# The last four routing tiles of a two-layer cross-attention kernel taken step by step together

## The chip, the cores and the metric

One Trainium2 chip, one of its cores. The metric is device time in microseconds (us) of one execution of the whole kernel. The kernel before was timed three times.

## The reference

x has 2048 rows of 256 numbers, the context 1601 rows of 192. Layer 0 routes the context into x and passes the result through a gate; layer 1 is a block of self-attention, cross-attention and MLP. All of it is f32. The part that the change touches is layer 0 and the start of layer 1:

```python
tok = context @ W_proj + b_proj
attn = softmax(x @ tok.T / 16)
routed = attn @ tok
ps_n, in_n = ln(x), ln(routed)
u = sigmoid([ps_n, in_n] @ W_u + b_u)
r = sigmoid([ps_n, in_n] @ W_r + b_r)
cand = tanh([r * ps_n, in_n] @ W_n + b_n)
x1 = ln((1 - u) * x + u * cand)
h = ln(x1)                      # layer 1
q, k, v = h @ wq.T, h @ wk.T, h @ wv.T
...
```

Then come 16 heads of width 16 over 2048 keys, a cross-attention over the 1601 context rows, and an MLP of width 1024.

## The kernel before

The order of every engine's work is written out by hand, and engines wait for one another with counting semaphores. The 2048 rows are 16 **tiles** of 128 rows in 4 **chunks** of 512. Layer 0 runs as a pipeline of **slots**, one per tile. In the slots 0 to 15 TensorE makes scores and weighted context sums of a chunk (`l0_scores`, `l0_pv`), and among them, four slots behind, the steps of a tile:

- `route` (L1094, L1095): two accumulating matmuls give the routed row sums in PSUM bank 6.
- `norms` on VectorE (L1701 to L1714): reciprocal of the row sum, scaling of the routed rows (L1702), their statistics, an inverse root (`rsqrt`, L1496 to L1503: 3 small instructions and 3 times 3 more, each waiting for the one before, for up to three columns at once: the routed tile, the new state of an earlier one, the finished x1 of a third), then the normalised routed row (L1709) and the normalised x1 of a third tile (`XH1`, L1714).
- `hats` (L1103): four transposes into bank 3; `concat` on ScalarE (L792) puts them into `CF`.
- `gates` (L1113, L1116): 16 and 8 matmul records into bank 7; `reset` (L771) and `update` (L777) are their tanh on ScalarE, the vector `gates` (L1723, L1725) lie between.
- `candidate` (L1125) in bank 7 again, its bias on VectorE (L1746, `CZ`), its tanh on ScalarE (L799, `CD`), then the new state `E2` (L1750 to L1752) and its statistics (L1512, L1514).
- `finish` (L1734, L1736): x1 from the new state, and its statistics. `h_transposed` (L1024, bank 2) and `h_taken` (L736) turn the normalised x1 into `hF`, from which layer 1 projects.

The buffers `TR`, `RPS`, `UZ`, `TU`, `CZ`, `CD`, `E2` exist once, `CF` and `XHS` twice. Slots 16 to 22 have no more scores: there the last tiles run one after the other, slot by slot.

The projections of layer 1 (`qkv`) are ten entries for each chunk, numbered 10n to 10n+9: two k units, two v units, a q unit, the norm of k, the second q unit, two v units, the norm of q. A k or q unit (L1042) is one eighth of a key or query projection, 128 features of 512 rows; a v unit (L1039) one tile. `split` on ScalarE evicts a k or q unit in three passes (L674, L675, L676: value, rounded value, square) and VectorE makes the lower part (`lower_parts`, L1536), after which GpSimd stores both. The squares buffer `SQ` has two halves, one for each unit of a pair. So a split first waits until the norm (L926) of the pair before has read them:

```python
wait(act, S["norms"], u // 2)
```

VectorE takes the norm of k (L1542, `k_norm`) and that of q (L1672, L1673). After the last norm of k it makes the row of shifts for the first queries (`self_shift(0)`, L1656 to L1519). Chunk 0 is projected behind slot 10, chunk 3 behind slot 22 (`DENSE`), chunks 1 and 2 in parts within the slots 16 to 21 (`EARLY`, `LATE`). Units 10 and up rotate over the PSUM banks 0, 1, 4, 5.

Behind all that `decide` computes a flag (L1834 to L1839, with L1228 on TensorE). TensorE loads it as a number and branches (`general`), and then starts the scores of the self-attention (L1308). GpSimd stores the parts of all chunks first and then the four rows of shifts; SyncE loads the keys and the first queries as those arrive.

Of the kernel before, what the change touches and what calls it, by code (L numbers as in the profile page):

```python
# [14 lines left out]
P = 128  # L15
# [116 lines left out]
def build(nc, ctx, d, out):  # L132
# [87 lines left out]
    TU = m.put("TU", [P, D], F32, oWOP + 3 * D * 4)  # L220
    PS = ctx.enter_context(nc.psum_tensor("PS", [P, 8, CHUNK], F32))
# [21 lines left out]
    AGX, NYX, MXP, NMX = 192, 224, 256, 272  # L243

    def sm(o, n=1, p=P):
# [10 lines left out]
        l0_scores l0_exp l0_lo l0_pv l0_oc l0_routed l0_hat l0_hatT l0_concat  # L256
# [44 lines left out]
    for n in range(CHUNKS):  # L301
        vs = [("v", kt, 0, 0) for kt in range(n * TPC, (n + 1) * TPC)]
        ks, qs = ([(kind, n * CHUNK, CHUNK, mm) for mm in range(2)] for kind in "kq")
        norms = [("norm", CHUNKS + 2 * n + i, CHUNK, 0) for i in range(2)]
        stage3.append([(10 * n + i,) + e for i, e in
                       enumerate(ks + vs[:2] + qs[:1] + norms[:1] + qs[1:] + vs[2:] + norms[1:])])
# [6 lines left out]
    DENSE = {10: 0, 22: 3}  # L313
    FIRST, SECOND = stage3[1], stage3[2]
    EARLY = {16: FIRST[0:4], 17: FIRST[8:10], 21: SECOND[8:10]}
    LATE = {16: FIRST[4:8], 19: SECOND[0:4], 20: SECOND[4:8]}
    SLOTS = TILES + TPC + 3
# [293 lines left out]
    def _(gp):  # L611
# [30 lines left out]
        for i in range(CHUNKS):  # L642
# [6 lines left out]
        for i in range(CHUNKS):  # L649
            store_shift(i, 0, i * CHUNK)  # L650
# [15 lines left out]
    def _(act):  # L666
# [99 lines left out]
        def reset(i):  # L766

            act.wait_ge(S["l0_gates"], i + 1)
            wait(act, S["l0_rps"], i)
            for c in range(2):  # L770
                ins = act.activation(TR[:, c, :], PS[:, 7, c * P:(c + 1) * P], ACT.Tanh, bias=sm(BRH + c), scale=0.5)  # L771
            ins.then_inc(S["l0_rtanh"], 1)

        def update(i):

            act.wait_ge(S["l0_ubiased"], i + 1)
            act.activation(TU[:], UZ[:], ACT.Tanh, scale=0.5)  # L777

        def state_hat(i):
# [5 lines left out]
            act.activation(XHS[:, i % 2, 0, :], X[:, i, :], ACT.Identity, scale=sm(NYX + i), bias=sm(NMX + i))  # L785

        def concat(i):

            act.wait_ge(S["l0_hatT"], i + 1)
            for k, (g_, b_) in enumerate(2 * [("L0_xattn_g_state", "L0_xattn_beta_state")]  # L790
                                         + 2 * [("L0_xattn_g_input", "L0_xattn_beta_input")]):
                ins = act.activation(CF[:, i % 2, k, :], PS[:, 3, k * P:(k + 1) * P], ACT.Identity,  # L792
# [3 lines left out]
        def candidate(i):  # L796

            act.wait_ge(S["l0_candz"], i + 1)
            act.activation(CD[:], CZ[:], ACT.Tanh).then_inc(S["l0_cand"], 1)  # L799

        def slot(k):
# [4 lines left out]
            if b >= CHUNKS:  # L806
                if k == TILES:
                    routed_out(b - 1)
                if g is not None:
                    reset(g)  # L810
                qkv(EARLY.get(k, ()))
                if g is not None:
                    update(g)
                state_hat(tile_at(k, 3))
                if r is not None:
                    concat(r)
                if g is not None:
                    candidate(g)
                qkv(LATE.get(k, ()))
                if h is not None:  # L820
                    h_taken(h)
                return
# [26 lines left out]
            else:  # L849
                if j == TPC - 1 and b + 1 < CHUNKS:  # L850
                    shift_row(b + 1)
                state_hat(tile_at(k, 3))
# [7 lines left out]
        for k in range(SLOTS):  # L860
            slot(k)
            if k in DENSE:
                qkv(stage3[DENSE[k]])

# [56 lines left out]
    def _(pe):  # L921
# [164 lines left out]
        def route(i):  # L1086
# [6 lines left out]
            wait(pe, S["l0_hat"], i)  # L1093
            pe.matmul(PS[:, 6, 0:D + 1], OC[:, 0, tt * P:(tt + 1) * P], WN[:, 0, :], start=True, stop=False)  # L1094
            pe.matmul(PS[:, 6, 0:D + 1], OC[0:SUM + 1, 1, tt * P:(tt + 1) * P], WN[0:SUM + 1, 1, :],  # L1095
                      start=False, stop=True).then_inc(S["l0_routed"], 1)

        def hats(i):
# [3 lines left out]
            for k in range(4):  # L1102
                ins = pe.transpose(PS[:, 3, k * P:(k + 1) * P], XHS[:, i % 2, k // 2, (k % 2) * P:(k % 2 + 1) * P],  # L1103
                                   ident[:])
            ins.then_inc(S["l0_hatT"], 1)

        def gates(i):

            pe.wait_ge(S["l0_concat"], i + 1)
            wait(pe, S["l0_candz"], i)  # L1110
            for mm in range(2):
                for c in range(4):
                    pe.matmul(PS[:, 7, mm * P:(mm + 1) * P], W0[:, 1, c, mm * P:(mm + 1) * P], CF[:, i % 2, c, :],  # L1113
                              start=(c == 0), stop=(c == 3))
            for c in range(4):
                ins = pe.matmul(PS[:, 7, D:2 * D], CF[:, i % 2, c, :], W0[:, 0, c, :], start=(c == 0), stop=(c == 3))  # L1116
            ins.then_inc(S["l0_gates"], 1)

        def candidate(i):
# [3 lines left out]
            pe.wait_ge(S["l0_rps"], i + 1)  # L1123
            for c in range(4):
                ins = pe.matmul(PS[:, 7, 0:D], RPS[:, c, :] if c < 2 else CF[:, i % 2, c, :], W0[:, 2, c, :],  # L1125
                                start=(c == 0), stop=(c == 3))
            ins.then_inc(S["l0_candps"], 1)

        def slot(k):
# [4 lines left out]
            if b >= CHUNKS:  # L1134
                if k == TILES:
                    for i in range(LAG):
                        l0_pv(n - LAG + i)
                    route(r)
                if g is not None:
                    gates(g)  # L1140
                qkv(EARLY.get(k, ()))
                if r is not None:
                    hats(r)
                if g is not None:
                    candidate(g)
                if tile_at(k, 3) is not None:
                    route(r + 1)
                qkv(LATE.get(k, ()))
                if h is not None:
                    h_transposed(h)  # L1150
                return
# [57 lines left out]
        for k in range(SLOTS):  # L1209
            slot(k)  # L1210
            if k in DENSE:
                if DENSE[k] == 0:
                    pe.wait_ge(S["saw_loaded"], 64)
                qkv(stage3[DENSE[k]])
# [878 lines left out]
```

## Time and profile before

| | us |
|---|---|
| three runs | 1514.67, 1515.40, 1518.74 |
| median | 1515.40 |
| the profiled execution | 1512.68 |
| its span, first to last instruction | 1511.0 |
| TensorE busy | 1409.6 (93%) |
| VectorE busy | 567.5 (38%) |
| ScalarE busy | 1094.8 (72%) |
| last layer 0 sum ends, by the span's clock | 322.8 |
| first self-attention score starts | 435.2 |
| mean granted clock of TensorE | 0.968 |

The span is the time between the first and the last recorded instruction; 1.7 us of the execution lie outside it. The granted clock is a share of full speed. Rows of a timeline give the start (us from the span's start), the busy time (us), the engine, the line, the operation, what it writes and reads, its size and count, and in square brackets the idle time of the engine before it with what ended that.

### The profile page before, as it was taken

What the parts mean: (1) busy time and instruction counts of PE and PEld (TensorE: products, weight loads), DVE (VectorE), ACT (ScalarE), POOL (GpSimd) and SP (SyncE); (2) the same over time, 40 slices, a digit from 0 to 9 for tenths busy, and PEclk for the clock granted to TensorE, in tenths of its full rate; (3) what the DMA queues carried; (4) which work ended last, traced back from release to release, by engine and by line L of the source; (5) the groups of instructions that cost most, each with busy time, mean ns of one, the idle gap of its engine ahead of it and who ended that gap; (6) DMA issues with size and microseconds to landing.
All of it is one profiled execution on the core that took longest, in us unless ns stands there. A gap on an engine that the chain in (4) does not pass through costs nothing.

```text
span 1511.0 us, 20524 instructions
## 1 busy us (share of the span) xinstructions
PE 1409.6 (93%) x7934; PEld 623.1 (41%) x7934; DVE 567.5 (38%) x1343; ACT 1094.8 (72%) x1346; POOL 48.7 (3%) x63
## 2 busy tenths in 40 slices
PE   7989899996679999999999998998999999999988
PEld 5668676775422223223222322322323432432347
DVE  5557575777540113303322231440431233143132
ACT  2543444453359999998999998888877787788842
POOL 2000000010010000000000000000000000000000
PEclk9999999998789999999999999999899999999998
DMA  9410001001269000100100353501000000000000
GB/s 298 164 37 1 1 1 56 1 29 51 88 125 148 22 13 12 39 14 15 34 28 12 44 119 48 122 29 47 12 12 15 22 12 12 22 15 1 4 11 14
DMA packets 35048, 66.05 MB, mean 44 GB/s; under 512 B 6203, under 2 KB 20093, under 8 KB 34205
## 3 DMA queue, kind: packets, MB, share of 16 engines
q1 hardware_dynamic: 29580, 43.24, 13.3%
q0 software_dynamic: 5360, 21.37, 3.9%
q8 instruction: 69, 1.13, 0.3%
q14 instruction: 39, 0.31, 0.1%
HBM read 42.70 MB, written 22.02 MB: 43 GB/s over the span
## 4 chain that ended last, share of the span: by engine, by line
PE 67%; ACT 21%; DVE 6%; issue 3%; DMA 2%; SPq 0%; DVEq 0%; POOL 0%; ACTq 0%; POOLq 0%
PE PS L1325 20%; ACT PX L886 19%; PE PS L1308 14%; PE PS L1376 4%; PE PS L1386 3%; PE PS L1361 2%; PE PS L1113 2%; PE PS L1125 2%; PE PS L1116 2%; PE PS L1042 2%; PE PS L1081 1%; PE PS L1082 1%; PE PS L1083 1%; PE PS L1344 1%; PE PS L1459 1%
## 5 line engine op out<-in xcount | busy, mean ns | idle before, releaser
L886 ACT ACTIVATE PX<-PS 128x1024 f32<-128x1024 f32 (+1 forms) x928 | 882.6, 1039 | 136.0 <-PE PS L1308 87.9
L1325 PE MATMUL PS<-PX,V 128*32 128x512 f32 (+1 forms) x3712 | 500.7, 612 | 5.0 <-ACT PX L886 3.0
L1308 PE MATMUL PS<-QST,stack 50*128 50x512 f32 (+1 forms) x1856 | 386.0, 474 | 19.6 <-issue 13.7
L1308 PEld LDWEIGHTS PS<-QST,stack 50*128 50x128 f32 (+1 forms) x1856 | 157.0, 185 | 417.5 <-ACT PX L886 335.5
L1882 DVE COPY OT<-PS 128x512 f32<-128x512 f32 x32 | 22.1, 691 | 310.5 <-PE PS L1325 309.3
L1325 PEld LDWEIGHTS PS<-PX,V 128*32 128x32 f32 (+1 forms) x3712 | 73.9, 108 | 151.3 <-issue 129.3
L755 ACT ACTIVATE PH<-PS 128x512 fp32r<-128x512 f32 (+1 forms) x52 | 31.2, 600 | 79.4 <-PE PS L1062 69.3
L1386 PE MATMUL PS<-W,HIDT 128*128 128x256 f32 x192 | 51.5, 414 | 9.8 <-ACT HIDT L872 9.8
L1376 PE MATMUL PS<-HC,W 128*128 128x512 f32 x96 | 53.2, 641 | 0.0
L1909 DVE RECIPROCAL REC<-REC 128x256 f32<-128x256 f32 x30 | 52.6, 1753 | 1.0
L771 ACT ACTIVATE TR<-PS,small 128x128 f32<-128x128 f32 x32 | 10.0, 363 | 56.7 <-PE PS L1116 56.7
L1386 PEld LDWEIGHTS PS<-W,HIDT 128*128 128x128 f32 x192 | 36.5, 200 | 34.5 <-issue 30.0
L1954 DVE TENSOR_SCALAR HIDT<-PS,cols 128x512 f32<-128x512 f32 x24 | 18.0, 751 | 79.9 <-PE PS L1376 79.8
L1694 DVE TENSOR_TENSOR PL<-PEXP,PH 128x512 fp32r<-128x512 f32 (+1 forms) x52 | 35.8, 689 | 27.2 <-ACT PEXP L756 26.1
L1081 PE MATMUL PS<-PH,CN 128*128 128x512 f32 (+1 forms) x104 | 43.2, 416 | 0.9 <-DVE PL L1694 0.9
L1932 DVE TENSOR_TENSOR XH<-PS,rows 128x256 f32<-128x256 f32 x28 | 11.9, 425 | 81.2 <-PE PS L1361 81.2
L1082 PE MATMUL PS<-PH,CN 128*128 128x512 f32 (+1 forms) x104 | 41.5, 399 | 0.0
L1083 PE MATMUL PS<-PL,CN 128*128 128x512 f32 (+1 forms) x104 | 41.4, 398 | 0.0
L1587 DVE TENSOR_REDUCE small<-PS 128x1 f32<-128x512 f32 x64 | 35.1, 570 | 8.2 <-PE PS L963 7.4
L1959 DVE TENSOR_TENSOR XH<-PS,rows 128x256 f32<-128x256 f32 x12 | 5.1, 425 | 78.2 <-PE PS L1386 78.2
L1042 PE MATMUL PS<-hF,SAW 128*128 128x512 f32 x64 | 31.5, 627 | 2.0 <-ACT hF L736 2.0
L792 ACT ACTIVATE CF<-PS,cols 128x128 f32<-128x128 f32 x64 | 24.0, 456 | 10.6 <-PE PS L1103 10.6
(194 smaller groups left out, 1461.6 us busy)
## 6 DMA issues: line engine op xcount, KB each, us to landing
QST<-q_parts SPq DMA_DIRECT2D x192, 64.0 KB
q_parts<-PARTS POOLq DMA_DIRECT2D x16, 512.0 KB, 3.6
stack<-k_parts SPq DMA_DIRECT2D x24, 200.1 KB, 6.7
stack<-k_parts SPq DMA_DIRECT2D x18, 256.0 KB
k_parts<-KPARTS POOLq DMA_DIRECT2D x8, 512.0 KB, 3.2
v_cross<-V POOLq DMA_DIRECT2D x1, 3328.0 KB, 12.3
V<-v_cross SPq DMA_DIRECT2D x2, 1664.0 KB, 13.7
k_parts<-PARTS POOLq DMA_DIRECT2D x6, 512.0 KB, 3.4
```

Source lines behind the costliest of these rows:

```text
L886: act.activation(PX[0:kr, (2 * t + half) % 4, :, :], PS[0:kr, slot:slot + 2, :], ACT.Exp, scale=SCALE).then_inc(at["exp"], 1)
L1042: ins = pe.matmul(PS[:, bank, :], SAW[:, "qk".index(kind), c, mm * P:(mm + 1) * P], hF[:, c, at:at + w], start=(c == 0), stop=(c == 1))
L1081: pe.matmul(PS[0:w, bank, :], c_hi, hi, start=first, stop=False)
L1082: pe.matmul(PS[0:w, bank, :], c_lo, hi, start=False, stop=False)
L1083: ins = pe.matmul(PS[0:w, bank, :], c_hi, lo, start=False, stop=last)
L1308: ins = pe.matmul(PS[0:kr, 2 * (n % LOOK) + jj, :], KST[a][lo:lo + NROW, pair, kt * P:kt * P + kr].bitcast(F32R), QST[lo:lo + NROW, pair, ...
L1325: ins = pe.matmul(PS[32 * j:32 * j + 32, 6, :], V[0:kr, kt, 2 * (g // 2 * GH + j) + g % 2, :], PX[0:kr, (2 * t + j // 2) % 4, j % 2, :], s ...
L1376: ins = pe.matmul(PS[:, 7, :], (CAWQ if kind == "u" else W1)[:, c, i * P:(i + 1) * P], HC[:, c, :], start=(c == 0), stop=(c == 1))
L1386: ins = pe.matmul(PS[:, 7, 0:D], HIDT[:, k, i * P:(i + 1) * P], W2[:, k, :], start=(k == 0), stop=(k == HID // P - 1))
L1587: ve.tensor_reduce(sm(MXP + tt * len(pcs) + p), PS[:, max_bank(m), 0:pcs[p][1]], AX, ALU.max) \
L1694: ve.tensor_tensor(PL[0:kr, n % RING, :].bitcast(F32R), PEXP[0:kr, n % RING, :], PH[0:kr, n % RING, :], ALU.subtract).then_inc(S["l0_lo"], 1)
L1909: ch(ve.reciprocal(part, part))
```

## The change

Slots 16 to 22 are replaced on every engine by a function `last_tiles` in which the tiles 12 to 15 go through each step together or close together. Their buffers (`CF4`, `XHS4`, `TR4`, `RPS4`, `TU4`, `CD4`, `E4`) exist four times, in the place of the context. Tile j of the four has a PSUM bank of its own for `route`, `gates` and `candidate` (6, 4, 5, 7). The statistics of the routed rows are made straight from PSUM, one inverse-root chain serves six columns, and ScalarE writes the normalised routed rows from PSUM. The new states of all four have one chain, and so have the four x1.

The projections of the chunks 1 and 2 have only the banks 0 and 1. The norm of k of chunk 1 stands behind `gates` of the last tile. In chunk 3 the values stand last, the norm of k comes forward by two units, and GpSimd stores the first row of shifts ahead of the last queries.

```diff
+        entries = ks + vs[:2] + qs[:1] + norms[:1] + qs[1:] + vs[2:] + norms[1:]
+        if n == CHUNKS - 1:
+            entries = ks + qs[:1] + norms[:1] + qs[1:] + vs[:2] + norms[1:] + vs[2:]
-    DENSE = {10: 0, 22: 3}
-    FIRST, SECOND = stage3[1], stage3[2]
+    DENSE = {10: 0}
+    FIRST, SECOND, THIRD = stage3[1:]
-        return (0, 1, 2, 3)[u % 4] if u < 10 else (0, 1, 4, 5)[u % 4]
+        return (0, 1, 2, 3)[u % 4] if u < 10 else u % 2 if u < 30 else (0, 1, 4, 5)[u % 4]
...
+                if half and i == CHUNKS - 1:
+                    store_shift(0, 0, 0)
```

ScalarE's new order:

```diff
+            a, b, c, e = LASTS
+            routed_out(CHUNKS - 1)
+            reset(a - 1)
+            update(a - 1)
+            for i in LASTS:
+                state_hat(i)
+            candidate(a - 1)
+            qkv(FIRST[0:1])
+            h_taken(a - 3)
+            qkv(FIRST[1:4])
+            for i in LASTS:
+                routed_hat(i)
+            concat(a)
+            concat(b)
+            reset(a)
+            update(a)
+            concat(c)
+            h_taken(a - 2)
+            reset(b)
+            update(b)
+            h_taken(a - 1)
+            candidate(a)
+            concat(e)
+            qkv(FIRST[4:5])
+            reset(c)
+            update(c)
+            candidate(b)
+            reset(e)
+            update(e)
+            qkv(FIRST[5:])
+            candidate(c)
+            candidate(e)
+            qkv(SECOND[0:6])
+            for i in LASTS:
+                h_taken(i)
+            qkv(SECOND[6:])
+            qkv(THIRD)
```

TensorE's:

```diff
+            for i in range(LAG):
+                l0_pv(STEPS - LAG + i)
+            gates(a - 1)
+            for i in (a, b, c):
+                route(i)
+            candidate(a - 1)
+            qkv(FIRST[0:1])
+            route(e)
+            h_transposed(a - 3)
+            qkv(FIRST[1:4])
+            hats(a)
+            hats(b)
+            gates(a)
+            hats(c)
+            h_transposed(a - 2)
+            gates(b)
+            h_transposed(a - 1)
+            candidate(a)
+            hats(e)
+            qkv(FIRST[4:5])
+            gates(c)
+            candidate(b)
+            gates(e)
+            qkv(FIRST[5:])
+            candidate(c)
+            candidate(e)
+            qkv(SECOND[0:6])
+            for i in LASTS:
+                h_transposed(i)
+            qkv(SECOND[6:])
+            qkv(THIRD)
```

VectorE's, with the two new helpers:

```diff
+        def routed_stats(i):
+            j = i - FIRST_LAST
+            ve.wait_ge(S["l0_routed"], i + 1)
+            ch(ve.reciprocal(sm(RS4 + j), PS[:, route_bank(i), D:D + 1]))
+            stats(PS[:, route_bank(i), 0:D], j, ch, STAT4, AG4)
...
+            for _ in range(2):
+                ch(ve.tensor_tensor(var, var, sm(RS4, TPC), ALU.mult))
+            rsqrt4(TPC + 2)
+            ch(ve.tensor_tensor(sm(SC4, TPC), sm(NY4, TPC), sm(RS4, TPC), ALU.mult))
+            ve.scalar_tensor_tensor(out=sm(SB4, TPC), in0=mean, scalar=-1.0, in1=sm(SC4, TPC), op0=ALU.mult,
+                                    op1=ALU.mult).then_inc(S["l0_scaled"], 1)
...
+            four = [(j, STAT4, AG4) for j in range(7)]
+            norms(None, a - 2, a - 3)
+            finish(a - 2, into=four[5])
+            gates(a - 1)
+            routed_stats(a)
+            routed_stats(b)
+            candidate_sum(a - 1)
+            routed_stats(c)
+            new_state(a - 1, four[4])
+            qkv(FIRST[0:1])
+            routed_stats(e)
+            routed_scales()
+            next_hat(a - 2, AG4 + 10, NY4 + 5)
+            finish(a - 1, AG4 + 8, NY4 + 4, four[6])
+            qkv(FIRST[1:4])
+            rsqrt4(1, 6)
+            next_hat(a - 1, AG4 + 12, NY4 + 6)
+            gates(a)
+            gates(b)
+            candidate_sum(a)
+            qkv(FIRST[4:5])
+            new_state(a, four[0])
+            gates(c)
+            candidate_sum(b)
+            new_state(b, four[1])
+            gates(e)
+            qkv(FIRST[5:])
+            candidate_sum(c)
+            new_state(c, four[2])
+            candidate_sum(e)
+            new_state(e, four[3])
+            rsqrt4(TPC)
+            qkv(SECOND[0:2])
+            for j, i in enumerate(LASTS):
+                finish(i, AG4 + 2 * j, NY4 + j, four[j])
+                qkv(SECOND[2 + j:3 + j])
+            rsqrt4(TPC)
+            for j, i in enumerate(LASTS):
+                next_hat(i, AG4 + 2 * j, NY4 + j)
+            qkv(SECOND[6:])
+            qkv(THIRD)
```

(a, b, c, e are the tiles 12, 13, 14, 15; `gates` and `candidate` on TensorE, and `reset`, `update`, `concat` on ScalarE, are as before but for buffers and banks.)

## Rows read from the trace of the kernel before

**Rows 1.** The page's first line.
```profile
span 1511.0 us, 20524 instructions
```

**Rows 2.** Windows: stretch, PE, PEld, DVE, ACT, POOL busy us (count), clock, DMA share, GB/s.
```profile
397.40:411.50 14.10, 3.19 (x12) 1.46 (x10) 10.77 (x39) 3.88 (x9) 1.45 (x2) 0.62 0.56 174
...
322.80:435.20 112.40, 76.09 (x316) 52.79 (x316) 73.50 (x225) 42.14 (x91) 13.24 (x15) 0.86 0.23 77
```

**Rows 3.** Timeline of slot 17 and the start of slot 18, VectorE and ScalarE.
```profile
354.50 0.42 DVE L1746 TENSOR_TENSOR CZ<-PS,rows 128x256 f32<-128x256 f32 x1 [1.27 <-PE PS L1125]
...
355.48 0.42 DVE L1750 TENSOR_TENSOR E<-CD,X 128x256 f32<-128x256 f32 x1 [0.55 <-ACT CD L799]
...
357.75 0.17 DVE L1701 RECIPROCAL small<-PS 128x1 f32<-128x1 f32 x1
357.95 0.48 DVE L1702 TENSOR_SCALAR E<-PS,small 128x256 f32<-128x256 f32 x1
358.58 0.43 DVE L1512 BATCH_NORM_STATS2 small<-E 128x6 f32<-128x256 f32 x1
...
359.38 0.17 DVE L1496 TENSOR_SCALAR small<-small 128x3 f32<-128x3 f32 x1
...
361.77 0.41 DVE L1709 TENSOR_SCALAR XHS<-E,small 128x256 f32<-128x256 f32 x1
...
363.59 0.48 DVE L1734 SCALAR_TENSOR_TENSOR E<-E,small,rows 128x256 f32<-128x256 f32 x1
...
363.94 1.48 ACT L792 ACTIVATE CF<-PS,cols 128x128 f32<-128x128 f32 x4
...
365.31 0.18 DVE L1514 BATCH_NORM_AGGREGATE small<-small 128x2 f32<-128x6 f32 x1
```

**Rows 4.** Timeline: ScalarE's split of the first query unit of chunk 1.
```profile
339.06 0.69 ACT L674 ACTIVATE PARTS<-PS,cols 128x512 f32<-128x512 f32 x1 [2.26 <-PE PS L926]
...
340.22 0.69 ACT L676 ACTIVATE SQ<-PS,cols 128x512 fp32r<-128x512 f32 x1
```

**Rows 5.** The chain that ended last: start, us, what, records merged.
```profile
334.16 1.73 PE PS L1125 x8
...
336.76 1.72 PE PS L1042 x4
...
341.75 1.79 PE PS L1113 x16
343.53 1.74 PE PS L1116 x8
```

**Rows 6.** Windows of 2 us around an idle TensorE (columns as in rows 2).
```profile
360.00:362.00 2.00, 0.00 (x0) 0.00 (x0) 1.69 (x10) 0.00 (x0) 0.00 (x0) 1.00 0.00 0
...
364.00:366.00 2.00, 2.00 (x6) 1.55 (x6) 1.17 (x4) 1.43 (x5) 0.00 (x0) 0.50 0.00 0
```

**Rows 7.** Timeline: the turn of tile 15 at low clock, and chunk 3.
```profile
409.83 0.69 PE L1024 MATMUL PS<-ident,XH 128*128 128x128 f32 x2 [4.24 <-DVE XH L1714]
...
411.57 5.08 PE L1042 MATMUL PS<-hF,SAW 128*128 128x512 f32 x8 [1.05 <-ACT hF L736]
```

**Rows 8.** Timeline: norm of k, shifts, values, the flag, the first score.
```profile
423.28 0.68 DVE L1542 TENSOR_REDUCE small<-PS 16x1 f32<-16x512 f32 x1
...
426.50 0.69 DVE L1536 TENSOR_TENSOR PARTS<-PARTS 128x512 fp32r<-128x512 f32 x1
427.23 0.76 DVE L1683 TENSOR_TENSOR V<-PS,rows 128x256 f32<-128x256 f32 x2
...
430.43 0.14 DVE L1839 TENSOR_SCALAR flag<-small 1x1 int32<-1x1 f32 x1
...
435.20 0.96 PEld L1308 LDWEIGHTS PS<-QST,stack 50*128 50x128 f32 x6 [5.13 <-issue]
```

**Rows 9.** The same turn into the cross-attention: flag, first score.
```profile
938.30 0.14 DVE L1839 TENSOR_SCALAR flag<-small 1x1 int32<-1x1 f32 x1
...
943.10 0.96 PEld L1308 LDWEIGHTS PS<-QST,stack 50*128 50x128 f32 x6 [5.15 <-issue]
```

More of the change, by code:

```diff
@@ L220, in build, with state_of, work_of, route_bank @@
     TU = m.put("TU", [P, D], F32, oWOP + 3 * D * 4)
+    FIRST_LAST = TILES - TPC
+    s = Map(nc, oKST + 2 * T * 4, oV)
+    CF4 = s.new("CF4", [P, TPC, 4, P], F32)
+    XHS4 = s.new("XHS4", [P, TPC, 2, D], F32)
+    TR4 = s.new("TR4", [P, TPC, 2, P], F32)
+    RPS4 = s.new("RPS4", [P, TPC, 2, P], F32)
+    TU4 = s.new("TU4", [P, TPC, D], F32)
+    CD4 = s.new("CD4", [P, TPC, D], F32)
+    E4 = s.new("E4", [P, TPC, D], F32)
+    assert s.at <= oKST + 2 * T * 4 + 2 * 4 * 2 * LPAD + 4 * LT * 2 * CW
+    def state_of(i):
+        if i < FIRST_LAST:
+            return CF[:, i % 2], XHS[:, i % 2]
+        return CF4[:, i - FIRST_LAST], XHS4[:, i - FIRST_LAST]
+    def work_of(i):
+        if i < FIRST_LAST:
+            return tuple(x[:] for x in (TR, RPS, UZ, TU, CZ, CD, E2))
+        j = i - FIRST_LAST
+        return TR4[:, j], RPS4[:, j], TU4[:, j], TU4[:, j], CD4[:, j], CD4[:, j], E4[:, j]
+    def route_bank(i):
+        return 6 if i < FIRST_LAST else (6, 4, 5, 7)[i - FIRST_LAST]
+    def gate_bank(i):
+        return 7 if i < FIRST_LAST else route_bank(i)
     PS = ctx.enter_context(nc.psum_tensor("PS", [P, 8, CHUNK], F32))
@@ L776, in update @@
             act.wait_ge(S["l0_ubiased"], i + 1)
[L777 removed]
+            _, _, uz, tu, _, _, _ = work_of(i)
+            act.activation(tu, uz, ACT.Tanh, scale=0.5)
         def state_hat(i):
@@ L805, in slot @@
             n = LT * b + (3 * j + 1 if j else 0)
[L806 to L822, printed above, removed]
             def piece(n):
@@ L858, in slot @@
                 h_taken(h)
-        for k in range(SLOTS):
+        for k in range(TILES):
             slot(k)
@@ L1133, in slot @@
             n = LT * b + (3 * j + 1 if j else 0)
[L1134 to L1151, printed above, removed]
             if j == 0:
@@ L1207, in slot @@
             maxima(5)
-        for k in range(SLOTS):
+        for k in range(TILES):
             slot(k)
@@ L1753, in candidate, with rsqrt4, routed_scales @@
-            stats(E2[:], 0, ch)
+            candidate_sum(g)
+            new_state(g)
+        def routed_stats(i):
+            j = i - FIRST_LAST
+            ve.wait_ge(S["l0_routed"], i + 1)
+            ch(ve.reciprocal(sm(RS4 + j), PS[:, route_bank(i), D:D + 1]))
+            stats(PS[:, route_bank(i), 0:D], j, ch, STAT4, AG4)
+        def rsqrt4(n, first=0):
+            rsqrt(n, ch, ag=AG4 + 2 * first, y=sm(NY4 + first, n), tmp=TMP4)
+        def routed_scales():
+            pairs = sm(AG4, 2 * TPC).rearrange("p (n two) -> p n two", two=2)
+            mean, var = (pairs[:, :, i:i + 1].rearrange("p n o -> p (n o)") for i in range(2))
+            for _ in range(2):
[4 more added lines that the diff above has]
+                                    op1=ALU.mult).then_inc(S["l0_scaled"], 1)
+            ve.wait_ge(S["l0_scaled"], 1)
@@ L1759, in slot @@
             n = LT * b + (3 * j + 1 if j else 0)
-            if b >= CHUNKS:
-                norms(r, f, h)
-                gates(g)
-                finish(f)
-                qkv(LATE.get(k - 1, ()))
-                qkv(EARLY.get(k, ()))
-                candidate(g)
-                return
             if j == 0:
@@ L1818, in slot @@
                 x_stats((None, range(6, 12), range(12, 16))[k])
-        for k in range(SLOTS):
+        for k in range(TILES):
             slot(k)
```

123 lines of the change are left out of this document (79 added, 44 removed).

## The prediction

> **What bounds the kernel now.** I read the page for the size of the stage, then windows, the timeline and the chain that ended last. The span is 1511.0 us [rows 1]; 1.7 us of the 1512.7 us execution lie outside it. The change touches 322.8 to 435.2, between the last sum of layer 0 and the first score of self-attention: 112.4 us in which TensorE is busy 76.1, VectorE 73.5 and ScalarE 42.1 [rows 2]. No engine is full. Work passes between them, and in 397.4 to 411.5 VectorE works 10.8 of 14.1 us while TensorE has 3.2. What follows 435.2 keeps its code, so I compute only when the first score starts. A change of 0.3% (4.5 us) is about what a measurement can tell from none.
>
> **Prices.** On VectorE, from start to start: an elementwise step 0.46 (0.42 busy and the gap behind it); CZ starts at 354.50 and the step behind its tanh at 355.48, so sum, tanh and waits are 0.98; a new state with statistics 357.75 - 355.48 = 2.27; reciprocal 0.20, scaling 0.63, statistics 0.80, so 1.63 up to 359.38; a root chain 361.77 - 359.38 = 2.39, or 0.20 for each of its 12 instructions; a finish with its statistics 363.59 to 365.5 = 1.9; a normalisation 0.45; `concat` 1.5 [rows 3]. A split takes 340.91 - 339.06 = 1.85, its pitch is 1.72, a 128x512 pass in it 0.58 [rows 4]. TensorE at full clock: candidate 1.73, a k or q unit 1.72, gates 1.79 + 1.74 = 3.53 [rows 5]; I take 0.86 for a v unit (half), 0.44 for four turned blocks, 0.22 for two, and 0.47 for a norm, scaled from these by columns.
>
> **What goes.** Seven root chains (slots 16 to 22) become five: 4.8 us less on VectorE. Four scalings of 0.63 go and four normalisations of 0.45 move to ScalarE: 4.3 less. Six small scale instructions come, 1.0 more with the later start. So VectorE loses some 8 us of work. On TensorE nothing goes. Whether this shows depends on the new order, which I walk.
>
> **Step A, 322.8 to 339.4.** TensorE starts gates of tile 11 at once, which hides the copy of the sums (a gain of 1.2). VectorE is the bound: from 323.0 chain 2.4, normalisation 0.45, finish 1.9, two gate steps 0.92, two routed statistics 2.0, CZ 0.46, a third 1.0, new state 2.27, a lower part 0.73, the fourth 1.0, joint chain and scales 3.2; sum 16.3. A statistic read from PSUM has no row; 0.43 as from SBUF, bounds 0.3 and 0.7 (the 512-wide reduction from PSUM is 0.68 [rows 8]), so ±1 over four.
>
> The Trainium skill, "VectorE: DVE Perf Modes", section "The TRN2 errata — SBUF-src ops pay a fixed extra latency per instruction", gives a fixed part of 120 cycles for a source in PSUM against 58 for one in SBUF. By it the four statistics would be an estimated 0.3 us longer than I take them, and the sum +6.6.
>
> **Step B, to 343.8.** ScalarE makes four routed rows, 128x256 from PSUM: not shown before, at most 0.58 by the 512-wide pass [rows 4], at least half of it; I take 0.57, as the fixed part dominates. They stand ahead of the first `concat` (341.7 to 343.2), and the second `hats` waits for that.
>
> **Clock.** TensorE is idle from about 338 to 343.2 but for 0.44. After such a gap the clock falls: idle at 360 to 362, and 0.50 at 364 to 366 [rows 6], the 1.2 GHz level. Chunk 3 starts at that level too (5.08 us for 8 records whose full-clock price is 3.44 [rows 5, 7]): 1.6 lost. I charge 1.6 here, bounds 0 and 1.6.
>
> In all steps together the low clock costs 7.0 us of the sum below (B 1.6, E 1.6, F 1.2, G 2.6).
>
> **Step C, to 366.7.** TensorE is now full: gates 12 end near 349.0; then `hats` 0.44, turn 0.22, gates 3.53, turn 0.4, candidate 1.73, `hats` 0.44, the first query unit 1.72, gates 3.53, candidate 1.73, gates 3.53, norm of k 0.47: 17.7.
>
> **Step D, the added wait, to 377.5.** The split of that query unit waits for the norm of k, since it overwrites the squares. The trace shows the dependence: ScalarE's split was released by L926 after 2.26 us idle [rows 4]. Before, the norm followed its unit directly. Now two gates and a candidate (8.8 us) stand between. ScalarE could start at 357.9, but waits until 366.8. Queued behind it: `reset`, `update` of tile 14, tanh of 13, `reset` of 15. VectorE waits for the squares before its lower part, so from 355.9 to 368.6 it does nothing, with two new states behind it. Then it works alone: 0.73 + 2.27 + 0.92 + 0.98 + 2.27 + 0.92 + norm of k 0.7 = 8.8. TensorE has the second query unit to do and waits for bank 1, as there are two banks, until 377.5.
>
> **Step E, to 392.0.** Behind the gap TensorE runs at low clock: two v units and a norm take 3.8 instead of 2.2, to 381.4, one candidate to 383.1. Then VectorE: CZ and tanh 0.98, state 2.27, CZ and tanh 0.98, state 2.27, chain 2.4.
>
> **Step F, to 407.3.** Two lower parts 1.46, four finishes 7.7, two v 0.76, lower part 0.73, norm of k 0.7, chain 2.4, and 1.2 for a split held by bank and clock (bounds 0, 1.6): 14.9 to 15.3.
>
> **Step G, to 420.4.** Normalisation 0.45; four turns through bank 2, each waiting for the eviction before. One took 409.83 to 411.57 with the next start [rows 7], so 1.6 to 1.74: 5.6 with the last eviction beside the unit. The query unit at low clock 3.4; split 1.9, v unit 0.86, lower part and v on VectorE, norm: 3.5. Chunk 3 starts at 420.4, where it started at 411.6 before [rows 7].
>
> **Step H, the new chunk order.** At full clock two k units and splits, norm, split of q, lower part: 8.45. Then VectorE: norm of k to shift rows 426.50 - 423.28 = 3.22, lower part 0.73, a v pair 0.76, and from the last v pair over the norm of q to the flag 430.57 - 427.23 = 3.34 [rows 8]. Sum 16.5; before, 19.0 from 411.57. From flag to score TensorE needs 435.20 - 430.57 = 4.63 [rows 8]. At the cross-attention the same gap is 943.10 - 938.44 = 4.66 [rows 9], so it is the load and branch, not the shift row; storing that earlier gains 0. First score: 420.4 + 16.5 + 4.6 = 441.5.
>
> **Sum.** 441.5 - 435.2 = +6.3; I take +6. On the profiled 1512.7 that is 1518.7; the median of the runs is 2.7 above it, so 1521.4.
>
> **Rivals.**
> - *Same* (1518.4): the clock stays full in steps B and F, and the PSUM statistics are short: +6.3 less 1.6, 1.2 and 0.5 = +3. For it: these two gaps are the short ones of the five, and a matmul stands in the first. Against: behind the gap at 360 the clock did fall [rows 6].
> - *Faster* (1510.5): the wait of step D does not bite, since VectorE and ScalarE get their work done under TensorE's full stretch. Norm of k would then be taken at 368.5 instead of 377.5, and the low stretch behind it goes: 9 + 1.6. The first score comes at 430.9, -4.3, with small gains -5. It decides if the eviction waits under 1 us for the norm. Against: the norm's place in TensorE's order. I leave room for a longer chain of the old slots being hidden that I misread.
> - *Start by the shift row*: the flag is not the bound. Then the early store pays 2 us: +4, 1519.5, at the edge of same. Against: rows 8 and 9 agree to 0.03 us.
> - *The change does nothing*: excluded, tiles 12 to 15 run through it.
>
> **Chances.** Forecast (slower by 4.5 to 9) 0.55, slower by more, with each unseen latency over 60 steps adding, 0.05; same, by the two rivals for it, 0.24; faster 0.16. The range goes from 1510 (the faster rival inside) to 1527 (all upper bounds: +1 and +1 in A and B, +2 in latencies over the forecast): 0.1 is left below, 0.07 above.
>
> **What would show it.** Right: ScalarE's split of the first query unit of chunk 1 waits 8 to 9 us for L926; VectorE idles some 12 us there; TensorE has gaps of 7 us before the second v unit and before the turns of the last tiles, with granted clock 0.50 behind them; chunk 3 starts 8 to 9 us later and takes 2 to 3 us less to the flag; flag to score stays 4.6. Wrong: the split waits under 2 us, chunk 3 starts before 412, or the score follows the flag in other than 4.6 us. If the stage is as computed and the time is not, a stall in the attention's first chunk (keys loaded at other times) did it.

## The result, and the profile after

| us | before | after |
|---|---|---|
| median of 7 runs each, side by side | 1517.4 (1513.7 to 1519.2) | 1530.3 (1525.8 to 1534.6) |
| profiled execution | 1512.7 | 1532.4 |
| last sum of layer 0 to first score | 112.4 [rows 2] | 129.3 |

The ratio is 1.010 (95% interval 1.0082 to 1.0118, which is 12 to 18 us); the medians lie 12.9 us apart. Forecast was slower by 6, with 1521.4 and a range up to 1527; measured was slower by more. Almost all of it lies in the stage that the prediction walks. What comes behind the first score takes 1078.2 us instead of 1075.8. Its code is the same in all thirteen kernels of this document, and their profiles give 1072.7 to 1079.1 us for it, so this difference says nothing.

Below, the page of the changed kernel: its span and busy times.

```profile
span 1530.8 us, 20493 instructions
...
PE 1421.2 (93%) x7934; PEld 628.1 (41%) x7934; DVE 563.5 (37%) x1315; ACT 1096.9 (72%) x1350; POOL 48.7 (3%) x63
```

VectorE is busy 4.0 us less than before, although one instruction among them is held for 3.1 us (step A below), and the time is longer. Now the windows of the changed kernel (columns as in rows 2): the first line answers to the last of [rows 2]; then the stretch called step C, the one of step D, and one ahead of the four turns.

```profile
323.40:452.70 129.30, 84.44 (x318) 55.88 (x316) 69.64 (x197) 44.58 (x96) 13.27 (x15) 0.80 0.22 72
346.10:374.00 27.90, 25.07 (x138) 21.72 (x138) 7.77 (x26) 11.51 (x31) 0.72 (x1) 0.88 0.10 33
374.00:385.30 11.30, 2.04 (x6) 0.71 (x5) 7.26 (x17) 4.94 (x12) 0.72 (x1) 0.89 0.13 48
408.00:417.30 9.30, 1.03 (x3) 0.12 (x1) 5.62 (x21) 1.84 (x3) 0.72 (x1) 0.50 0.43 131
```

TensorE's busy time in the stage rises from 76.1 to 84.4 us for 318 instead of 316 records: the same work at a mean granted clock of 0.80 instead of 0.86. In the third line only 2.0 of 11.3 us have a matmul: step D. In the fourth the clock is at its lower level, 0.50, while VectorE works.

The steps of the prediction, each as a length between the same marks, in us:

| step | predicted | measured | excess |
|---|---|---|---|
| A, to the routed rows on ScalarE | 16.6 | 22.7 | 6.1 |
| B, to the end of the gates of tile 12 | 9.6 | 10.4 | 0.8 |
| C, to the end of the norm of k | 17.7 | 17.5 | -0.2 |
| D, to the second pair of v units | 10.8 | 11.2 | 0.4 |
| E | 14.5 | 15.3 | 0.8 |
| F | 15.3 | 16.4 | 1.1 |
| G, to the start of chunk 3 | 13.1 | 13.3 | 0.2 |
| H, to the flag | 16.5 | 16.9 | 0.4 |
| flag to score | 4.6 | 5.5 | 0.9 |
| sum | 118.7 | 129.2 | 10.5 |

**Step D** is there as it was forecast. The timeline of the changed kernel, ScalarE, VectorE and TensorE:

```profile
374.14 0.69 ACT L709 ACTIVATE PARTS<-PS,cols 128x512 f32<-128x512 f32 x1 [9.11 <-PE PS L999]
...
376.09 0.69 DVE L1635 TENSOR_TENSOR PARTS<-PARTS 128x512 fp32r<-128x512 f32 x1 [12.90 <-ACT SQ L711]
...
385.26 3.78 PE L1112 MATMUL PS<-SAW,hF 128*128 128x256 f32 x8 [7.24 <-DVE small L1641]
```

The split waits 9.11 us for the norm (L999 here, L926 before), VectorE idles 12.90, and TensorE has a gap of 7.24 with the low clock behind it: 3.78 us for two v units whose full-clock price is 1.72.

**Step A** is not as forecast. The timeline of the changed kernel at its beginning, all engines:

```profile
323.41 0.58 ACT L798 COPY OC<-PS 128x512 f32<-128x512 f32 x1 [1.43 <-PE PS L1156]
323.44 3.51 POOL L678 MEMSET V<- 128x4096 f32 x1 [82.49 <-PE PS L1156]
323.45 0.18 DVE L1613 BATCH_NORM_AGGREGATE small<-small 128x2 f32<-128x6 f32 x1
323.67 3.30 DVE L1595 TENSOR_SCALAR small<-small 128x3 f32<-128x3 f32 x1
...
327.00 0.17 DVE L1596 TENSOR_SCALAR small<-small 128x3 int32<-128x3 int32 x1
...
332.52 2.08 PE L1205 MATMUL PS<-W,RPS 128*128 128x256 f32 x4 [3.03 <-DVE RPS L1830]
...
332.82 0.43 DVE L1611 BATCH_NORM_STATS2 small<-PS 128x6 f32<-128x256 f32 x1
...
334.39 1.91 PE L1205 MATMUL PS<-W,CF 128*128 128x256 f32 x4
...
336.42 0.42 DVE L1850 TENSOR_TENSOR CZ<-PS,rows 128x256 f32<-128x256 f32 x1 [1.74 <-PE PS L1205]
...
341.09 0.69 DVE L1635 TENSOR_TENSOR KPARTS<-KPARTS 128x512 fp32r<-128x512 f32 x1 [0.86 <-ACT SQ L711]
```

The first step of the root chain, three numbers in each partition, takes 3.30 us instead of 0.17 and ends 0.02 us after GpSimd's fill of half of `V`. The same fill ran in the kernel before at the same point. There VectorE had nothing to do at first, and its root chain came behind the fill. The timeline of the kernel before, VectorE and GpSimd:

```profile
322.83 3.51 POOL L645 MEMSET V<- 128x4096 f32 x1 [82.52 <-PE PS L1083]
...
325.37 0.48 DVE L1702 TENSOR_SCALAR E<-PS,small 128x256 f32<-128x256 f32 x1
326.00 0.43 DVE L1512 BATCH_NORM_STATS2 small<-E 128x6 f32<-128x256 f32 x1
...
326.79 0.17 DVE L1496 TENSOR_SCALAR small<-small 128x3 f32<-128x3 f32 x1
```

Scaling and statistics under the fill have their usual 0.48 and 0.43 us. The root chain begins 0.45 us after it has ended.

**Theory one.** A third or more of the loss is this fill: it holds the root chain for 3.1 us, TensorE then idles 3.03 us ahead of the candidate, and its clock falls, so that the candidate takes 3.78 instead of 1.73. VectorE then waits 1.74 us for the candidate and 0.86 us for the squares of the key unit behind it. The wait of step D is the other, larger part. **Rivals:** the long record is a slow first instruction of a chain for another reason; or the new order itself, and not one wait, costs what step D shows.

The Trainium skill, "SBUF — State Buffer", section "Who interferes with whom", says that VectorE and GpSimd share one pair of SBUF ports as a lock: a `tensor_scalar` with both ends in SBUF can take a mode that needs it, and whoever issues second is blocked until the first instruction is done, while an instruction with two inputs in SBUF does not collide with one of GpSimd that only writes there, as a fill does. The rows above agree with the first half (3.30 us against 0.17), and experiment 7 tries the second.

### The profile page after: what moved, and what is told of

It is laid out like the page before. It is cut to its first block, busy times and chain, and to the rows that moved or that the text cites. A ratio compares the mean times of both kernels' runs of the same rounds, so it can differ in the third digit from the quotient of the medians.

```text
span 1530.8 us, 20493 instructions
## 1 busy us (share of the span) xinstructions
PE 1421.2 (93%) x7934; PEld 628.1 (41%) x7934; DVE 563.5 (37%) x1315; ACT 1096.9 (72%) x1350; POOL 48.7 (3%) x63
## 3 DMA queue, kind: packets, MB, share of 16 engines
q8 instruction: 69, 1.13, 0.3%
## 4 chain that ended last, share of the span: by engine, by line
PE 67%; ACT 22%; DVE 7%; issue 3%; DMA 1%; SPq 0%; DVEq 0%; ACTq 0%; POOLq 0%
PE PS L1424 20%; ACT PX L959 19%; PE PS L1407 14%; PE PS L1475 4%; PE PS L1485 3%; PE PS L1460 2%; PE PS L1192 2%; PE PS L1195 2%; PE PS L1205 1%; PE PS L1154 1%; PE PS L1155 1%; PE PS L1156 1%; PE PS L1115 1%; PE PS L1443 1%; PE PS L1558 1%
## 5 line engine op out<-in xcount | busy, mean ns | idle before, releaser
L1686 DVE TENSOR_REDUCE small<-PS 128x1 f32<-128x512 f32 x64 | 35.1, 570 | 10.8 <-PE PS L1036 10.0
L1192 PEld LDWEIGHTS PS<-CF,W 128*128 128x128 f32 x256 | 32.6, 200 | 2.2 <-issue 0.5
```

What stands on the lines that cost most here:

```text
L1192: pe.matmul(PS[:, bank, mm * P:(mm + 1) * P], W0[:, 1, c, mm * P:(mm + 1) * P], cf[:, c, :], start=(c == 0), stop=(c == 3))
```

## The experiments

All were compared with runs of the kernel before on the same chip; its medians there are 1517.4 for the experiments 1 to 4, 1515.4 for 5 to 8 and 1515.3 for 9 to 11. The ratio is worked out from all runs and need not equal that of the two medians. The experiments 5, 6, 7 and 10 have one run each and are read by their profiles. "Stage" is the time from the copy of the last sums to the first score, in the profiled execution. Line numbers shift by a few between kernels.

### 1. The fill later

```diff
-            if i == 1:
-                gp.wait_ge(S["l0_pv"], STEPS)
-                gp.memset(V[:, TILES // 2:TILES], 1.0)...
             for half, dst in enumerate((kd[0], qd[0])):
+                if i == 1 and half:
+                    gp.wait_ge(S["l0_pv"], STEPS)
+                    gp.wait_ge(S["l0_cand"], FIRST_LAST + 1)
+                    gp.memset(V[:, TILES // 2:TILES], 1.0)...
```

> The changed kernel, but GpSimd fills the second half of V (3.51 us) only after the candidate's tanh of tile 12, behind the key stores of chunk 1. Theory one: in the changed kernel the fill, which starts 0.23 us before VectorE's first root step, holds that instruction for 3.30 us instead of 0.17, and TensorE, idle 3.03 us for it, then runs its candidate and a key unit at low clock (3.78 and 2.81 us instead of 1.73 and 1.72). Without the collision the instruction takes 0.17 us and all that is gone: 3.1 + 2.0 + 1.1 = 6.2 us, so about 1524 us against 1530.3. Theory two: the long instruction has another cause, or its delay is taken up again in the wait for the norm: under 1 us, 1530.

Median 1526.9 (1523.2 to 1529.0), ratio to before 1.0064 (1.0045 to 1.0083); stage 122.8. The stage is 6.5 us shorter than the changed kernel's, for 6.2 expected; the median is only 3.4 lower. Step A takes 17.0 us instead of 22.7, where 16.6 was predicted. The candidate of tile 11, in the timeline of this kernel, has its full-clock length and no wait:

```profile
327.17 1.13 PE L1206 MATMUL PS<-W,RPS 128*128 128x256 f32 x4
328.14 1.03 PE L1206 MATMUL PS<-W,CF 128*128 128x256 f32 x4
```

The fill now runs at 355.35, where VectorE waits in step D anyway.

### 2. The norm of k straight behind its unit

```diff
-            qkv(FIRST[4:5])
+            qkv(FIRST[4:6])
...
-            qkv(FIRST[5:])
+            qkv(FIRST[6:])
```

(in `last_tiles` of TensorE, ScalarE and VectorE)

> The changed kernel, but the norm of k of chunk 1 stands directly behind the first query unit on all engines, as in the kernel before. Theory one: ScalarE's split no longer waits 9.1 us and VectorE no longer idles 12.9 us; by my walk the second v pair is reached 9 us sooner and the low clock behind the 7.2 us gap goes: 9 to 11 us less, about 1520. Theory two: VectorE and TensorE have to do the same work anyhow and TensorE's full stretch sets the end: the norm's wait for the squares shifts the idle time only, under 3 us, 1528 or more.

Median 1521.5 (1515.1 to 1526.5), ratio 1.0028 (1.0012 to 1.0045); stage 119.4, 9.9 shorter than the changed kernel's. Timeline, ScalarE's split and VectorE's lower part:

```profile
364.69 0.69 ACT L709 ACTIVATE PARTS<-PS,cols 128x512 f32<-128x512 f32 x1 [0.36 <-PE PS L999]
...
366.64 0.69 DVE L1635 TENSOR_TENSOR PARTS<-PARTS 128x512 fp32r<-128x512 f32 x1 [4.16 <-ACT SQ L711]
```

The split waits 0.36 instead of 9.11 us and VectorE 4.16 instead of 12.90. The rest of the order is that of the change, so these 9.9 us are the price of one wait and not of the order as such.

### 3. Both

> Both edits in one kernel. If they are separate causes the gains add: 6 + 10 = 16 us, about 1514, which is below the kernel before (1517.4). If one hides the other: no better than the better of the two alone, 1520.

Median 1514.8 (1511.2 to 1518.1), ratio 0.9981 (0.9968 to 0.9994); stage 112.9, that is 16.4 less than 129.3. The two shares are 6.5 + 9.9 = 16.4: they add, more exactly than single profiles can promise. By the medians it is 3.4 and 8.8 alone and 15.5 together, by the ratios 5.5, 10.9 and 18.1. With one edit on each, the changed kernel's stage is back at 112.9, against the 112.4 of the kernel before.

### 4. The kernel before, with chunk 3's values last and the shift row stored early

```diff
-        stage3.append([... enumerate(ks + vs[:2] + qs[:1] + norms[:1] + qs[1:] + vs[2:] + norms[1:])])
+        entries = ks + vs[:2] + qs[:1] + norms[:1] + qs[1:] + vs[2:] + norms[1:]
+        if n == CHUNKS - 1:
+            entries = ks + qs[:1] + norms[:1] + qs[1:] + vs[:2] + norms[1:] + vs[2:]
+        stage3.append([(10 * n + i,) + e for i, e in enumerate(entries)])
...
+                if half and i == CHUNKS - 1:
+                    store_shift(0, 0, 0)
```

> The kernel before with one part of the change alone: in chunk 3 the values stand last, the norm of k comes two units sooner and the first row of shifts is stored ahead of the last queries. Theory one: from chunk 3's first unit to the flag 16.5 us instead of 19.0, the score follows the flag by 4.6 us as before: 2.5 us less, about 1515. Theory two, the score waits for the row of shifts: the early store makes it 4 us less, and flag to score falls below 4 us. Theory three: the order of chunk 3 is worth nothing.

Median 1514.7 (1512.3 to 1520.0), ratio 0.9992 (0.9977 to 1.0007): the median is 2.7 lower, but the interval holds both no change and the 2.5 us expected. The stage is 115.3 us in this profile, 2.9 longer than before, of which 2.5 lie in the slots, whose code is unchanged. Chunk 3 to flag took 18.6 us (19.0 before), the 2.5 expected are not there in the profile: my 19.0 held 1.6 of low clock, and the k units run at low clock here too. And from the end of the flag to the first weight load it took 5.41 us instead of 4.63. Timeline, VectorE and TensorE's weight loads:

```profile
432.68 0.14 DVE L1843 TENSOR_SCALAR flag<-small 1x1 int32<-1x1 f32 x1
...
438.23 0.96 PEld L1312 LDWEIGHTS PS<-QST,stack 50*128 50x128 f32 x6 [5.92 <-issue]
```

So in the profiles this third part of the change gains 0.4 and gives back 0.8; the runs tell neither.

### 5. The kernel before, with the fill moved onto its root chain

```diff
                 gp.wait_ge(S["l0_pv"], STEPS)
+                gp.wait_ge(S["l0_routed"], TILES - 3)
                 gp.memset(V[:, TILES // 2:TILES], 1.0)...
```

> The kernel before, but GpSimd's fill of V also waits for the routed rows of tile 12, so that it starts near 325.6 us and VectorE comes to its root chain (first instruction at 326.8) in the middle of it. Theory one, the fill holds back a tensor-scalar instruction with source and destination in SBUF: that first instruction ends with the fill, about 2.3 us instead of 0.17, while the scaling from PSUM and the statistics in front of it keep 0.48 and 0.43. Most of the delay lies beside a full TensorE there, so the time moves by 0 to 2 us. Theory two, the long instruction in the changed kernel is something of that kernel: 0.17 us here.

Timeline, GpSimd and VectorE:

```profile
328.55 3.51 POOL L646 MEMSET V<- 128x4096 f32 x1 [84.81 <-PE PS L1096]
328.73 0.48 DVE L1703 TENSOR_SCALAR E<-PS,small 128x256 f32<-128x256 f32 x1
329.36 0.43 DVE L1513 BATCH_NORM_STATS2 small<-E 128x6 f32<-128x256 f32 x1
...
330.15 1.93 DVE L1497 TENSOR_SCALAR small<-small 128x3 f32<-128x3 f32 x1
```

The same instruction of the kernel before is now held too, from its start to the end of the fill (332.08 against 332.06). The scaling from PSUM, a tensor-scalar instruction as well, is not. The stage stays at 112.5 and one run gave 1516.1: here a held chain lies beside a full TensorE and costs nothing.

### 6. Half of the fill at the old place

```diff
-                gp.memset(V[:, TILES // 2:TILES], 1.0)...
+                gp.memset(V[:, TILES // 2:3 * TILES // 4], 1.0)...
```

(the other half as in experiment 1)

> The changed kernel with the fill cut in two: one half at the old place (about 1.75 us), the other after the tanh of tile 12. Theory one: VectorE's first root step is held to the end of the first half, 1.5 us instead of 3.3, TensorE waits about 1.3 us before the candidate of tile 11 instead of 3.0 and keeps its full clock (1.73 us for it). Theory two, any fill costs the same: 3.3 us still.

Timeline, GpSimd, VectorE, TensorE:

```profile
324.77 1.80 POOL L678 MEMSET V<- 128x2048 f32 x1 [82.51 <-PE PS L1159]
325.00 1.59 DVE L1598 TENSOR_SCALAR small<-small 128x3 f32<-128x3 f32 x1
...
332.15 1.13 PE L1208 MATMUL PS<-W,RPS 128*128 128x256 f32 x4 [1.32 <-DVE RPS L1833]
```

Half the fill, half the stall. TensorE waits 1.32 us for the candidate and keeps its full clock; stage 124.0, one run 1528.4. Step A takes 18.5 us instead of 22.7. Of these 4.2 us, 1.7 are the shorter stall and the other 2.5 are the two waits of VectorE, for the candidate and for the squares of the key unit, which are gone with the low clock.

### 7. Another form for the first step of the root

```diff
-            link(ve.tensor_scalar(v, var, EPS, None, ALU.add))
+            link(ve.scalar_tensor_tensor(out=v, in0=var, scalar=EPS, in1=var, op0=ALU.add, op1=ALU.max))
```

> The changed kernel, where the first step of each root chain is a scalar-tensor-tensor with the variance as both inputs (same result) and no longer a tensor-scalar. Theory one, the form decides (one SBUF source streamed by a tensor-scalar is held by the fill, two inputs are not): the first step takes 0.2 us and the second, still a tensor-scalar, is held for 3.1 us instead; step A ends at the same time. Theory two, whatever VectorE issues first after the fill starts is held: the first step takes 3.3 us still.

Timeline, GpSimd and VectorE:

```profile
326.43 3.51 POOL L678 MEMSET V<- 128x4096 f32 x1 [82.45 <-PE PS L1156]
326.66 0.17 DVE L1595 SCALAR_TENSOR_TENSOR small<-small 128x3 f32<-128x3 f32 x1
326.86 3.10 DVE L1596 TENSOR_SCALAR small<-small 128x3 int32<-128x3 int32 x1
```

The stall leaves the instruction whose form was changed and goes to the next tensor-scalar. It is the form with source and result in SBUF that the fill holds, not the first step of a chain. Stage 127.1, one run 1530.6. The stage is 2.1 us shorter than the changed kernel's with nearly the same stall. TensorE waits 2.82 us here and is at the low clock for less of the candidate, which takes 3.0 us instead of 3.78:

```profile
335.30 1.27 PE L1205 MATMUL PS<-W,RPS 128*128 128x256 f32 x4 [2.82 <-DVE RPS L1830]
336.37 1.91 PE L1205 MATMUL PS<-W,CF 128*128 128x256 f32 x4
```

### 8. Experiment 3 with four banks for the units of chunk 2

```diff
-        return ... else u % 2 if u < 30 else (0, 1, 4, 5)[u % 4]
+        return ... else u % 2 if u < 20 else (0, 1, 4, 5)[u % 4]
```

> The kernel with both repairs (fill later, norm sooner; 1514.8 us), and the units of chunk 2 rotating over the banks 0, 1, 4 and 5. Theory: the first query unit of chunk 2 no longer waits 4.0 us for a value eviction and is no longer at low clock (3.78 us), the norm and the split behind it come before VectorE asks for them, which saves the 2.7 us that VectorE waits there: 2 to 3 us less, 1512. Rival: VectorE's chain of finishes sets the time there whatever the banks: under 1 us.

Median 1511.4 (1508.6 to 1514.6), ratio 0.9973 (0.9957 to 0.9989); stage 108.3, 4.6 less than in experiment 3, for 2 to 3 expected: the first query unit of chunk 2 no longer waits for a bank and keeps the full clock (1.88 us for its records, 3.78 with a wait of 3.99 ahead of it in experiment 3). The timeline of experiment 3, then that of this kernel:

```profile
387.48 3.78 PE L1116 MATMUL PS<-hF,SAW 128*128 128x512 f32 x4 [3.99 <-DVE V L1783]
...
394.18 0.69 DVE L1636 TENSOR_TENSOR PARTS<-PARTS 128x512 fp32r<-128x512 f32 x1 [2.67 <-ACT SQ L712]
```

```profile
383.26 1.88 PE L1116 MATMUL PS<-hF,SAW 128*128 128x512 f32 x4
...
393.48 0.69 DVE L1636 TENSOR_TENSOR PARTS<-PARTS 128x512 fp32r<-128x512 f32 x1
```

VectorE's wait of 2.67 us for that unit's split, which the changed kernel has too, is gone. TensorE's idle time gathers in one place instead, 14.10 us ahead of the turns.

### 9. And the last four turns through two banks

```diff
+    def turn_bank(i):
+        return 2 if i < FIRST_LAST else 2 + i % 2
...
-            take(2, S["ln1_taken"], i + 1)
+            bank = turn_bank(i)
+            take(bank, S["ln1_taken"], i + 1)
```

(and that bank in the two transposes and their eviction)

> The two earlier edits (fill later, norm of k sooner) and four banks for the units, and now the turns of tiles 12 to 15 alternate between banks 2 and 3. In the kernel with four unit banks these turns came at a pitch of 1.71 us, each waiting for the eviction before it. Theory one: the pitch is turn 0.22, semaphore and eviction on one bank; with two banks the next turn lies beside the eviction and ScalarE's eviction (about 0.8 us with its gap) sets the pitch. Three pitches lose about 0.8 us each, 2.4 us, of which most reaches the first query unit of chunk 2: stage from 108.3 to about 106, median 2 below that kernel's 1511.4, some 6 below before. Rival: VectorE's normalisations, which these turns read through two buffers, set the pitch too; then the four turns stay over 1.5 us apart and the stage stays at 108 to 108.5.

Median 1508.9 (1507.0 to 1510.4), ratio 0.9950 (0.9932 to 0.9967); stage 105.3. The turns, in the timeline of this kernel:

```profile
401.10 1.14 PE L1104 MATMUL PS<-ident,XH 128*128 128x128 f32 x4 [14.14 <-DVE XH L1824]
402.83 1.36 PE L1104 MATMUL PS<-ident,XH 128*128 128x128 f32 x4 [0.60 <-DVE XH L1824]
403.98 3.62 PE L1122 MATMUL PS<-hF,SAW 128*128 128x512 f32 x4
```

From the first turn to the query unit it takes 2.88 us, and took 5.61 in experiment 8. The third turn now waits 0.60 us for a normalised row of VectorE: the rival is right for that remainder.

### 10. The changed kernel with the shift row stored behind the queries again

```diff
-                if half and i == CHUNKS - 1:
-                    store_shift(0, 0, 0)
...
-        for i in range(1, CHUNKS):
+        for i in range(CHUNKS):
             store_shift(i, 0, i * CHUNK)
```

> The changed kernel with one edit: the shift row of chunk 0 is stored behind the two query stores of chunk 3 again, as it was. From flag to first score the changed kernel took 5.51 us, the one before 4.67. Theory one: the early store lets the queue of SP load the shift row and the keys before the flag is set, and this traffic stands beside TensorE's load of the flag and its branch; with the store back, SP's loads start 1.5 to 2 us later and the gap is 4.6 to 4.9. Rival one: the late store itself now sets the start; then the first score is released by a load, and the gap is over 5.5. Rival two: the gap belongs to the new order of chunk 3 (query stores just ahead of the flag), and it stays 5.4 to 5.6 with issue as its cause.

Timeline, VectorE, SyncE's queue, weight loads:

```profile
448.44 0.14 DVE L2015 TENSOR_SCALAR flag<-small 1x1 int32<-1x1 f32 x1
449.05 1.14 SPq L528 DMA_DIRECT2D QST<-shift  x4
450.29 5.50 SPq L498 DMA_DIRECT2D stack<-k_parts  x6
453.33 0.95 PEld L1405 LDWEIGHTS PS<-QST,stack 50*128 50x128 f32 x6 [5.25 <-issue]
```

From flag to first weight load it is 4.75 us, and was 5.51 in the changed kernel. There SyncE's loads lie ahead of the flag, in its own timeline:

```profile
445.31 1.15 SPq L528 DMA_DIRECT2D QST<-shift  x4
446.55 2.98 SPq L498 DMA_DIRECT2D stack<-k_parts  x6
...
446.98 0.14 DVE L2017 TENSOR_SCALAR flag<-small 1x1 int32<-1x1 f32 x1
...
452.63 0.95 PEld L1407 LDWEIGHTS PS<-QST,stack 50*128 50x128 f32 x6 [6.02 <-issue]
```

Theory one's forecast for this gap holds, and the late store does not bound the start. One run gave 1534.0, within the changed kernel's own range.

### 11. The same on the kernel of experiment 9

> The kernel with two turn banks, and the shift row stored behind the query stores again. Theory one (early traffic lengthens the gap from flag to score): the gap falls from some 5.2 to 4.6 to 4.9 and the median by 0.3 to 0.6 us, within what the runs tell apart. Rival one (late store bounds): slower by 0.5 to 1.5 us, gap over 5.5. Rival two (no part of it): the same gap and median.

Median 1507.4 (1502.3 to 1511.4), ratio 0.9947 (0.9927 to 0.9966); flag to first weight load 4.66 us instead of 5.21. The medians of 9 and 11 lie 1.6 us apart, but their ranges overlap, so the gain of this edit is shown by the gap alone. The nine kernels with the early store have 5.05 to 5.62 us in this gap, the four without it 4.63 to 4.75. That SyncE's key loads, then under way, slow the number's load or the branch is the reading that fits; which of the two, and by what, was not tried.

This kernel keeps the change's joint steps, root chains and buffers, and its order but for the norm of k, the fill and the store. It is some 8 us faster than the kernel before on the same chip, which the changed kernel missed by 12.9: some 21 us between the two. Its stage, as a window (columns as in rows 2):

```profile
320.60:425.50 104.90, 74.46 (x318) 51.86 (x316) 66.49 (x197) 44.62 (x96) 13.27 (x15) 0.86 0.25 83
```

VectorE has 7.0 us less work in it than in the kernel before (73.5), near the 8 that were computed for the idea, and the stage is 7.5 us shorter.

## Why the prediction was right in sign and short in size

**Right.** Steps C and D, the mechanism that the forecast rests on: the stretch with a full TensorE (17.7 for 17.5), the wait of the split for the norm of k and what is queued behind it (9 for 9.11; 12.7 idle for 12.90; 7 for 7.24). The gap before the turns is there as well, 8.31 us for 7, with the clock at 0.50. Experiment 2 shows that this wait costs 9.9 us of the stage, where the rival "faster", which needed just this wait gone, had 9 + 1.6. The rival's condition and its price are right; its stage of 108.1 is not reached (119.4, and 112.9 without the fill), since other terms were short. Four routed rows on ScalarE took 1.93 together where 4 times 0.57 was taken. Two chains fewer and the moved work gave VectorE 7.0 us less in the stage (experiment 11), where 8 were worked out.

The statistics from PSUM took 0.43, as taken from SBUF. But a reciprocal with its statistics took 1.11 from start to start where 1.0 was taken, so the four lie 0.4 over the sum. By the figures of the Trainium skill, "VectorE: DVE Perf Modes", section "The TRN2 errata — SBUF-src ops pay a fixed extra latency per instruction", it had been an estimated 0.3. The length of the statistics does not bear that out: 0.43 us from either memory.

**The step that failed is A**, "VectorE is the bound ... sum 16.3", and in it "chain 2.4". Each instruction was priced by a row in which GpSimd stood still. The change moves a root chain from behind GpSimd's fill to beside it, and the fill was not in the walk at all. The chain takes 5.5 us instead of 2.4, which is 3.1 directly. Then TensorE idles before the candidate, which the prediction had not foreseen, and at the low clock the candidate takes 3.78 instead of 1.73. VectorE, which bounds the step, waits 1.7 us for it and 0.8 for the key unit behind it, of which the walk had neither. With the 0.4 of the statistics that makes the 6.1 of the table. Experiments 1, 5, 6 and 7 carry it: later fill, no stall; fill moved in the kernel before, stall there; half fill, half stall; other form, stall on the next one. With the fill out of the way the walk's 118.7 us stand against 122.8 in experiment 1: the mechanism that was forecast is there, and 4.1 us are sizes.

**Sizes.** "Flag to score stays 4.6" was read from two places in which no key load runs ahead of the flag [rows 8, 9]; it is 5.5 with the early store, and "storing that earlier gains 0" should have had a loss as its other bound. In step H the 16.5 was nearly right (16.9), but the 19.0 that it was set against held 1.6 us of low clock. Step F is 1.1 over because VectorE waits 2.67 us for the split of the query unit, where 1.2 with an upper bound of 1.6 was charged. The timeline of the changed kernel:

```profile
404.39 3.78 PE L1115 MATMUL PS<-hF,SAW 128*128 128x512 f32 x4 [3.99 <-DVE V L1782]
...
411.10 0.69 DVE L1635 TENSOR_TENSOR PARTS<-PARTS 128x512 fp32r<-128x512 f32 x1 [2.67 <-ACT SQ L711]
```

Experiment 8 removes this wait. In step B the gates of tile 12 took 6.1 us where some 5.2 with the low clock was taken. In step E the two v units and the norm took 4.4 up to the candidate where 3.9 was taken. Together 4.4 us besides step A. The range also has a slip: the upper bounds that it names add up to 1525.4 and not to the 1527 that it gives. The measured time lies above both.

**Stage and total.** The profiled stage grew by 16.9 and the median by 12.9. One profile of a kernel is one execution: experiment 10, which has the same slots as the changed kernel, reached chunk 3 in 105.1 us where that took 106.8, since a k unit behind the gap ran 2.23 us there and 2.81 here. In the same way experiment 4 needed 2.5 us more for the slots than the kernel before, with the same code. So shares worked out from single profiles are good to some 2 to 3 us. The medians of experiments 1 to 3 (3.4, 8.8 and 15.5 less than the changed kernel) bear the same order as the stage's 6.5, 9.9 and 16.4; the two alone make 12.2, which is 3.3 short of both together and within the intervals.

## What to carry to other kernels

When work is moved in time, list what every other engine does in the stretch to which it goes, fills on GpSimd included: here a step on three numbers cost 3.3 us. If a buffer is guarded by a wait for an earlier reader, put that reader straight behind its producer on its own engine, since whatever is issued between them becomes the wait of all that is queued behind. And when a reordering comes out slower, look for single waits before it is dropped: two edits gave back 16.4 of the stage's 16.9 us, and bank edits made the new order the faster one.

## What the runs showed of the hardware that was not expected

- A VectorE `tensor_scalar` from SBUF to SBUF that starts during a GpSimd fill ends within 0.02 us of the fill, for both sizes tried: 3.30 and 3.10 us under one of 3.51, 1.93 under the rest of one, 1.59 under one of 1.80, and 0.17 without. `tensor_scalar` from PSUM (0.48), the statistics (0.43) and `scalar_tensor_tensor` (0.17) under the same fill kept their lengths.
- TensorE's clock at the same candidate, in two groups of four records: behind 1.32 us of idling both have the length of the 2.4 GHz level (1.13 and 1.03 us). Behind 2.82, 3.04 and 3.03 us the first group took 1.27, 1.67 and 2.08 us and the second 1.91 each time, with a mean granted clock of 0.65, 0.57 and 0.50 over the candidate: the second group is at the 1.2 GHz level, and the first is so in part or in whole (experiments 7 and 10 and the changed kernel).
- TensorE's way from a flag to the branch's first weight load takes 4.63 to 4.75 us in four kernels, and 5.05 to 5.62 in the nine in which SyncE's key loads start ahead of the flag.
